# One VectorE instruction instead of two for the row maxima of a pair of score chunks in an attention layer

## The reference

```python
xf = x.reshape(Bb, Cc, N)                       # 2 images, 32 channels, N = 4096 pixels
f1 = jnp.einsum('oc,bcn->bon', w1, xf) + b1[None, :, None]
f2 = jnp.einsum('oc,bcn->bon', w2, xf) + b2[None, :, None]
f3 = jnp.einsum('oc,bcn->bon', w3, xf) + b3[None, :, None]
A = jax.nn.softmax(jnp.einsum('bcn,bcm->bnm', f1, f2), axis=-1)
out = jnp.einsum('bcm,bnm->bcn', f3, A) + xf
```

## Time and profile before

| | |
|---|---|
| median of 3 runs | 1288.99 us |
| lowest and highest run | 1287.61 and 1912.49 us |
| the profiled execution's own time | 1288.67 us |
| its span, first to last instruction | 1286.7 us |
| TensorE busy | 1171.4 us (91%), 7126 matmuls |
| VectorE busy | 988.2 us (77%) |
| ScalarE busy | 661.2 us (51%) |
| GpSimd busy | 492.0 us (38%) |
| mean granted TensorE clock | 0.949 of full |

### The profile page before, as it was taken

One profiled execution on the slowest core, in us unless ns is written; L12 is line 12 of the kernel. 1 busy time (PEld: TensorE's weight loads), 2 busy tenths in 40 slices (PEclk: granted clock), 3 DMA queues, 4 the chain that ended last, 5 costly groups with the idle time before them and its releaser, 6 DMA issues.

```text
span 1286.7 us, 20328 instructions
## 1 busy us (share of the span) xinstructions
PE 1171.4 (91%) x7126; PEld 494.0 (38%) x7126; DVE 988.2 (77%) x1679; ACT 661.2 (51%) x882; POOL 492.0 (38%) x537
## 2 busy tenths in 40 slices
PE   4999997688999999979899888988998999999996
PEld 1788884144544444423232222222222222222221
DVE  6699998875767666678788889888767777777772
ACT  4876765855555444222353453444654455554453
POOL 7000000037777777777777777774000000000000
PEclk9999998799999999955699999999999999999998
DMA  2655550058454441111121111111000000000000
GB/s 54 143 130 115 114 115 1 1 168 235 125 175 135 142 126 54 51 46 51 52 53 50 51 51 51 51 51 33 1 1 1 1 17 1 0 0 0 0 1 16
DMA packets 59672, 79.21 MB, mean 62 GB/s; under 512 B 12230, under 2 KB 43974, under 8 KB 59414
## 3 DMA queue, kind: packets, MB, share of 16 engines
q1 hardware_dynamic: 44342, 47.03, 14.1%
q0 software_dynamic: 15264, 31.29, 8.7%
HBM read 70.94 MB, written 7.34 MB: 61 GB/s over the span
## 4 chain that ended last, share of the span: by engine, by line
PE 49%; POOL 19%; DVE 14%; issue 11%; ACT 4%; SPq 1%; DMA 1%; DVEq 1%; POOLq 0%; ACTq 0%
POOL tile_data L554 19%; PE psum L1971 13%; PE psum L1953 9%; PE psum L1994 8%; PE psum L1718 6%; DVE maxes L1144 4%; PE psum L1733 3%; DVE probs_and_weighted L881 3%; PE psum L1668 2%; PE psum L1745 2%; PE psum L2000 2%; DVE probs_and_weighted L891 1%; PE psum L1916 1%; ACT quads L1574 1%; PE psum L1736 1%
## 5 line engine op out<-in xcount | busy, mean ns | idle before, releaser
L554 POOL DMA_INDIRECT tile_data<-quad_table,index_u x477 | 468.2, 982 | 390.2 <-DMA quad_table<-quad_rows_or_splits 245.1
L1144 DVE TENSOR_REDUCE maxes<-psum 128x1 f32<-128x512 f32 x512 | 326.0, 681 | 93.9 <-PE psum L1953 92.3
L1574 ACT ACTIVATE quads<-psum 128x1024 f32<-128x1024 f32 x256 | 248.1, 1021 | 248.6 <-PE psum L2000 248.6
L1971 PE MATMUL psum<-quads 128*64 128x512 f32 x1024 | 256.8, 610 | 0.0
L1833 PE MATMUL psum<-scratch,quad_rows_or_splits 128*128 128x512 f32 (+1 forms) x486 | 210.7, 574 | 5.9 <-DVE scratch L966 5.9
L1994 PE MATMUL psum<-quads,probs_and_weighted 32*128 32x512 f32 x1024 | 147.9, 647 | 2.2 <-ACT quads L1574 1.5
L1833 PEld LDWEIGHTS psum<-scratch,quad_rows_or_splits 128*128 128x128 f32 x486 | 88.3, 193 | 103.0 <-issue 87.6
L1953 PE MATMUL psum<-products_or_attention 128*128 128x512 bf16 x256 | 91.3, 419 | 36.2 <-DVE maxes L1144 36.2
L978 DVE TENSOR_TENSOR probs_and_weighted<-psum,quads 128x512 f32<-128x512 f32 (+1 forms) x81 | 51.2, 642 | 73.6 <-PE psum L1833 68.3
L1971 PEld LDWEIGHTS psum<-quads 128*64 128x64 f32 x1024 | 58.8, 136 | 120.4 <-issue 111.3
L1433 ACT ACTIVATE vals<-psum 96x384 f32<-96x384 f32 x53 | 25.8, 486 | 142.7 <-PE psum L1797 142.7
(11 more groups left out here) (227 smaller groups left out, 1400.8 us busy)
## 6 DMA issues: line engine op xcount, KB each, us to landing
products_or_attention<-positions SPq DMA_DIRECT2D x30, 576.0 KB, 8.1
products_or_attention<-bands SPq DMA_DIRECT2D x12, 768.0 KB, 7.5
tile_data<-quad_table,index_u POOLq DMA_INDIRECT x477
quads<-bands SPq DMA_DIRECT2D x6, 768.0 KB, 10.5
quad_table<-quad_rows_or_splits SPq DMA_DIRECT2D x4, 768.0 KB, 8.4
products_or_attention<-bands SPq DMA_DIRECT2D x4, 576.0 KB, 6.7
quad_table<-quad_rows_or_splits SPq DMA_DIRECT2D x2, 640.0 KB, 8.4
products_or_attention<-positions SPq DMA_DIRECT2D x4, 288.0 KB, 7.5
```

The source lines that it names most:

```text
L554: pool.indirect_dma_start(out=out[:, k * CORNERS * C:(k + 1) * CORNERS * C], out_offset=None, in_=table, in_offset=bass.IndirectOffsetOnAx ...
L1144: v.reduce_max(maxes[:, tile_of_q, block_of_k:block_of_k + 1], psum[:, FREE + c % 2, :], AXIS_X)\
L1574: act.activation(probs[:, s % 2, 2 * BLK * h:2 * BLK * (h + 1)], psum[:, SCORES + 2 * h:SCORES + 2 * h + 2, :].rearrange("p a n -> p (a n) ...
L1971: last = pe.matmul(psum[2 * C * h:2 * C * h + 2 * C, SUMS, :], f3[b][:, 4 * s + i, :], probs[:, s % 2, BLK * i:BLK * i + BLK], start=s == ...
```

## The change

A second function, `largest_of_pairs`, waits for both chunks of a pair and finds both sets of row maxima with one instruction over banks 5 and 6: 1024 columns in, 2 out. It counts `maxed` up by 2. `attend` calls it in all blocks without tiles, that is for sets 7 to 15; for sets 0 to 6 `largest` stays. `LAST_SCORED` is changed to even numbers. `score_chunks` and its waits stay.

```diff
 SCORED = [6, 6, 4, 4, 4, 4, 4, 0]
 MERGED_SCORED = [3, 7, 3, 7, 3, 6, 3, 0]
-LAST_SCORED = [0, 0, 6, 7, 7, 7, 5, 0]
+LAST_SCORED = [0, 0, 6, 6, 6, 8, 6, 0]
@@
+            def largest_of_pairs(b, j, chunks):
+
+                for c in chunks[::2]:
+                    tile_of_q, block_of_k = c // NBLK, c % NBLK
+                    v.wait_ge(chunk_scored, lin(queries(b, j), MAXIMA, c + 2))
+                    v.reduce_max(maxes[:, tile_of_q, block_of_k:block_of_k + 2], psum[:, FREE:FREE + 2, :], AXIS_X)\
+                        .then_inc(maxed, 2)
@@
-                    largest(b_next, nxt, range(c, c + scored_at[s]))
+                    (largest if tiles else largest_of_pairs)(b_next, nxt, range(c, c + scored_at[s]))
```

## The result

| | before | after |
|---|---|---|
| median | 1289.8 us | 1316.22 us (1314.5 to 1321.59, 4 runs) |
| profiled execution | 1288.67 us | 1315.29 us |
| its span | 1286.7 us | 1313.2 us |
| VectorE busy | 988.2 us, 1679 instructions | 979.8 us, 1535 instructions |

The ratio is 1.0218, with a 95% interval of 1.0177 to 1.0258; it compares the means and leaves out the one slow run of the kernel before (1912.49 us), which still counts in the median of 1289.8. The kernel became slower by about 2%, 26.6 us by the profiled executions. The forecast of 1309.8 us had the direction, the place and the mechanism, and 21.1 of the 26.6 us; the measured time is inside the range (1301 to 1319). It did not put the result on the side of the 2% line (1314.8 us) where the median fell; the interval holds values on both sides of that line.

What follows compares the result with a forecast made beforehand. TensorE was taken as the bound, its waits adding one for one. Sets 9 to 14 add 14.3 us, set 15 2.3, set 8 4.3, set 7 0.2: 21.1 on 1288.7 gives 1309.8 us, range 1301 to 1319.

Steps and rivals of the forecast that it cites:

- The price P: Duration of the new VectorE maxima instruction over 1024 columns: 1.22 us, from 0.69 plus 0.53 for 512 added columns.
- The loop: Shortest time from the start of one pair of chunks to the next: 1.93 us instead of 1.17.
- An ordinary block: Each block of sets 9 to 14 grows by 2.38 us; six blocks give 14.3 us.
- step 4: In sets 9 to 14, VectorE comes late behind a reciprocal and `read_fill`: 0.30 us more a block.
- the end: At a block's turning, the last pair's maxima end at 1.87 us after its start instead of 1.72: 0.16 us more.
- Set 8: With the changed table, 6.5 us of new waits less 2.2 us of old ones: 4.3 us more.
- Set 7: TensorE already waits for VectorE and slack takes up added delays: 0.2 us more, at most 1.3.
- Set 15: No new block of queries, so six step borders of 0.10 us and no late VectorE: 2.3 us more.
- Not slower: Rival: VectorE is the late engine and saves about 12 us of work; 1285 to 1289 us, chance 0.03.
- Two banks cost like two instructions: Rival: the new VectorE instruction lasts 1.36 us, 13 us more in all; 1322 us, chance 0.07.
- partly caught up: Rival: the banks' delay is partly absorbed by slack, so half of the sum; about 1299 us, chance 0.06.
- The clock falls: Rival: TensorE's lower busy share halves its clock, some 36 us for one set; chance 0.02 together with the unforeseen.

Runs made afterwards that it cites:

- the better kernel above: Kernel before with single maxima, set 8's table 2, 6, 6, 6, 6, 6 from step 1, new queries read between step 4's two pairs: 1286.61 us, ratio 0.9976.

## Why the prediction held, and where it was too small

**What bounds.** "TensorE is the bound, and whatever keeps it waiting is added to the time one for one": right. TensorE's waits for maxima and its time grew together, and what VectorE saved bought nothing. The prediction put that at 12 us; by busy time it is 7.9 (183.4 to 175.5).

**The price P.** 1.22 forecast from VectorE's own rows, 1.219 measured. By ScalarE's cheaper columns (P = 1.11) it would have been too low, and so by the estimate of 1.19 from the Trainium skill (VectorE: DVE Perf Modes, section on the errata). The upper end, 1.36, did not come.

**The loop, 0.65 + 1.22 + 0.06 = 1.93.** This is the step that was mis-sized, in its first term: 0.72 for 0.65, so 1.99. The prediction took the start of the maxima behind a chunk from an instruction that waits and counts in one, and costed the count of 2 at nothing. With a count of 1 the kernel took 1311.77 us, against a forecast of 1309.8, and its set 9 grew by 2.3 us, against 2.38. The resumption, 0.06, held, but for the waits inside TensorE's loop. Between the first chunk of set 7 and the last pair of set 15 the forecast is 20.9 us (21.1 less the 0.16 behind that pair) and the timeline 27.6, so 6.7 were missing: some ninety distances at 0.06 make 5.4, fifteen waits in the loop at 0.085 make 1.3, and set 15 has 0.36 once. That only 5.5 are missing between the profiled executions is luck: the changed one was 1.3 us shorter ahead of set 7.

**An ordinary block**, forecast 2.38 us, took 3.3 in sets 10 to 14. Four distances of 1.55 became 2.00 on average plus once 0.08 (1.9 for 1.51); borders of 1.83 became 1.99, one of them 2.08 (0.75 for 0.41); step 4 took 0.45 for 0.30 (0.02 of it a slip in the sum, where 3.42 + 1.22 is 4.64 and not 4.62), and the end 0.22 for 0.16. The places are all as named. Step 4 in the changed kernel, TensorE, answering to the earlier trace rows:

```profile
1138.89 0.60 PE L1961 MATMUL psum<-quad_rows_or_splits,tile_data 128*128 128x512 bf16 x2
...
1141.65 0.60 PE L1961 MATMUL psum<-quad_rows_or_splits,tile_data 128*128 128x512 bf16 x2 [0.29 <-DVE maxes L1152]
```

and VectorE, which came from the reading of the queries, answering to the earlier trace rows:

```profile
1138.75 0.93 DVE L1186 RECIPROCAL scratch<-scratch 32x128 f32<-32x128 f32 x1
1139.72 0.75 DVE L1103 SCALAR_TENSOR_TENSOR tile_data<-tile_data,keep_rest,psum 128x512 f32 x1
1140.38 1.22 DVE L1152 TENSOR_REDUCE maxes<-psum 128x2 f32<-128x1024 f32 x1
```

The end, answering to the earlier trace rows:

```profile
1154.93 0.40 PE L1968 MATMUL psum<-ident_h,nm_parts 128*128 128x128 bf16 x4 [0.64 <-DVE nm_parts L1173]
```

**Set 8** took 5.1 for 4.3: the same 0.06 at twelve distances. **Set 7** took 0.2, as forecast; the slack in front of the product for image 1 did take up the rest (2.88 us from pair to pair there, where it was 3.51). **Set 15** took 0.36 us more at one distance (2.35 in step 1), once. Its cause is open: a written-out loop on TensorE left it in place, and in the kernel with a count of 1 and the one with pairs in the blocks with tiles it is not there.

**The rivals.** "Not slower" was wrong, but its condition was right: the kernel with half the columns has a P of 0.69, under 0.84, and is not slower. The advice for large tiles that the prediction took beside it from the Trainium skill (VectorE: DVE Perf Modes, section on the errata) is given there for instructions that read SBUF; these maxima read PSUM. "Two banks cost like two instructions" and "partly caught up" did not come. "The clock falls" did not come in the changed kernel's profile; it did, for a few microseconds, in some of the experiments.

**The chances.** Slower by over 2% had 0.17, and the ratio is 1.0218, with the 2% line inside its interval. The forecast lay 5 us below the line, and an error of 0.06 us in one term, ninety times over, was enough to cross it. That 2% is about what a measurement of this kernel can tell from no change was wrong: the better kernel above differs by 0.24%, with an interval of 0.9967 to 0.9986.

## What to carry to other kernels

Where one engine fills two buffers and another empties them, reckon the loop from the start of a fill to the moment the same buffer can be filled again, and compare it with the distance at which the filling engine naturally comes back. Merging two reads makes the reader's work smaller and that loop longer (here 1.17 to 1.99 us); where the loop got longer than that distance the kernel lost, where it stayed under it nothing was lost, and where the reader was late it lost as well. No run here shows a merged read over full banks that gained. Count such an instruction's semaphore up by 1, and put the waits that remain where the engine has other work to do first.

## What the runs showed that I had not expected

- A VectorE instruction that counts a semaphore up by 2 had its wait in a separate instruction, and started 0.06 to 0.07 us later after its releaser than one that counts by 1.
- A TensorE wait inside an instruction that computes a register (in a loop) cost 0.08 us more than one attached to the weight load, once it really waited. In the kernel before the same instructions hid this.
- Short stretches at half of TensorE's clock came in several profiles. In the kernel with the count of 1 one began at 981.4 us, between the two 1.3 us waits of set 8's step 5:

```profile
970.00:980.00 10.00, 8.20 (x44) 1.68 (x42) 7.50 (x8) 6.35 (x6) 0.00 (x0) 1.00 0.00 0
981.50:991.00 9.50, 8.18 (x29) 1.54 (x29) 4.42 (x5) 1.50 (x2) 0.00 (x0) 0.50 0.00 0
```

  There some 10 us at 1.2 GHz and not 2.4 held set 8 up: it took 46.4 us, some 3.6 more than the 42.8 that its distances make (43.6 less 0.065 at each of twelve). The changed kernel has the same waits and shows none, and the kernel with pairs only where there is slack shows one at the start of set 9 with none of these waits (clock 0.66 from 993 to 998 us). What decides is open. Two of 3.4 us together cost 2.0 us in the kernel with the loop written out, one costs 1.5 us a set in the kernel with pairs in the blocks with tiles (51.6 against 50.1), and the one of 10 us costs 3.6 here. Medians are blurred by as much.
